# Layer norm split in two: the mean taken off a transposed copy of x, the reciprocal deviations applied to results

## The chip, the cores and the metric

The kernel runs on one core of a Trainium2 chip. TensorE (PE) multiplies matrices, VectorE (DVE), ScalarE (ACT) and GpSimd (POOL) work element by element, SyncE (SP) issues transfers. Each engine runs its own instructions in order and waits on semaphores; only transfers overlap freely. The metric is the device time of one execution in microseconds (us), the median of several runs; lower is better.

## What is computed

Two blocks, a linear attention and a gated feed-forward part with low-rank experts, read the same layer-normed tokens, and their results are added to x. There are 2048 tokens of 512 features; the feed-forward width is 1376, padded to 11 chunks of 128.

```python
def _layernorm(x, axis=-1, eps=1e-05):
    m = jnp.mean(x, axis=axis, keepdims=True)
    v = jnp.var(x, axis=axis, keepdims=True)
    return (x - m) / jnp.sqrt(v + eps)
...
xn = _layernorm(x)
# attention: Q = elu(xn Wq' + bq)+1, K likewise, V = xn Wv' + bv
out = (Q @ (K'V)) / (Q . sum(K) + 1e-8) @ Wo' + bo
# feed-forward: w = expert weights from sigmoid(xn W_router), the top 2
gate = xn @ W_gate + lora + expert_lora(w);  up = likewise
ffn = (silu(gate) * up) @ W_down + lora + expert_lora(w)
x = x + out + ffn
```

## The kernel before

Every product is made of float32 parts: an operand is rounded to a high part by ACT (`round_to`), DVE subtracts it for the low part (`sub`), and PE multiplies three times (high by high, high by low, low by high; lines 1245 to 1247).

**Stage 1** goes over 16 tiles of 128 tokens. For tile t, DVE takes mean and variance (`stats_of`, into `mv`), POOL makes the reciprocal deviation `rstd` in two instructions (`rstd_of`), and DVE writes the normed tile `xn` (`normalise`). PE turns it with four transposes (`transpose_tokens`, L1264) into one PSUM bank; ACT and DVE split that into `xt` (`tokens_hi`, `tokens_lo`), and `xt` is kept in DRAM (`scr_x`) for later stages. PE makes keys `k`, values `va` and the rest `vz`, DVE adds the key bias (`kb`), and so on. In the same tile POOL and DVE pass the expert choice of the tile before back and forth: POOL `rden` (L608), DVE `compare`, POOL `eq`, `gt`, `rank` (L611 to L615), then `rstd_of(t + 3)`, then seven small instructions up to `wtok` (L626), and `rden` of the next tile. DVE stands at `compare` until POOL's `rden` is there, and only behind it comes `tokens_lo(t + 1)`, which PE needs for the next tile.

**Queries.** Four groups of 512 tokens, each with four products `queries(g, c)` into two PSUM banks in turn. ACT reads the bank twice (`query_relus`, L757 and L759), makes an exponential (L764), and DVE adds (L1049). Then `denominators`, a DVE reciprocal of 3.35 us (`reciprocals`, L1091), ACT's rounding of it (`reciprocal_hi`), DVE's low part (`reciprocal_lo`, L1096), PE's `expand` (L1372), DVE's `scaled`, the low and high parts `qn_h`, `qn_l`, and `attention`. The last attention's products run behind the first gate product of the next stage.

**Feed-forward.** Four groups by 11 chunks: PE gate (14 products), up (14), down (14); ACT applies silu to the gate's bank, DVE multiplies by up (`hf`), and both split it.

The order of work on each engine is written out by hand; nothing reorders it.

## Time and profile before

| | |
|---|---|
| median of 3 runs | 669.52 us (669.11 to 671.9) |
| the profiled execution | 671.42 us, span 669.6 us |
| PE busy over the span | 98% |
| DVE, ACT, POOL busy | 56%, 38%, 19% |
| granted TensorE clock, mean | 0.997 |
| stage 1, queries, feed-forward end about at | 131, 228, 670 us |

A row of the timeline gives the start, the duration, engine, line, operation, output and inputs, and in brackets how long the engine had stood before it and what ended that. PE's matmuls overlap by some 0.16 us, so its pace is read from one start to the next.

### The profile page before, as it was taken

Reading aid. Unit: us, or ns where it says so; the run is one execution under the profiler, and the core shown is the slowest. Engines: PE = TensorE matmul, PEld = TensorE weight load, DVE = VectorE, ACT = ScalarE, POOL = GpSimd, SP = SyncE. Lnnn points to the kernel's source line nnn. Section 1 sums busy time; section 2 is a strip of 40 time slices with the busy share of each in tenths; the row PEclk is TensorE's granted clock in tenths of the full one; section 3 lists DMA queues with packets and bytes.
Section 4 is the critical chain, followed back from the end, with each engine's and each line's share of the span. In section 5 each row is a group of like instructions: output and inputs, shape, how many; then the busy total and the mean of one; then the engine's idle time right before and its main releaser. Section 6 shows DMA issues by size and latency. Waiting matters only on the chain.

```text
span 669.6 us, 10326 instructions
## 1 busy us (share of the span) xinstructions
PE 659.4 (98%) x3568; PEld 545.9 (82%) x3568; DVE 375.8 (56%) x698; ACT 257.5 (38%) x413; POOL 127.1 (19%) x290
## 2 busy tenths in 40 slices
PE   6999999999999999999999999999999999999998
PEld 5998999977777788888888888888888888888886
DVE  5677888778775956334345443445444326534433
ACT  4444454467235423323233333243233324323321
POOL 3466566626246230000000000000000000000000
PEclk8999999999999999999999999999999999999999
DMA  7875666644754679940025100011400001300001
GB/s 222 300 258 192 209 224 220 231 181 141 288 218 158 238 217 3 45 160 0 1 78 200 52 0 0 0 67 76 187 0 0 0 5 73 126 0 0 0 0 63
DMA packets 41642, 74.21 MB, mean 111 GB/s; under 512 B 19392, under 2 KB 20288, under 8 KB 39952
## 3 DMA queue, kind: packets, MB, share of 16 engines
q1 hardware_dynamic: 38672, 64.52, 34.6%
q10 hardware_dynamic: 2736, 9.05, 3.5%
q0 software_dynamic: 208, 0.30, 0.2%
q8 instruction: 16, 0.26, 0.2%
q14 instruction: 10, 0.08, 0.0%
HBM read 52.81 MB, written 21.04 MB: 110 GB/s over the span
## 4 chain that ended last, share of the span: by engine, by line
PE 94%; DVE 3%; DMA 1%; ACT 1%; issue 0%; SPq 0%; DVEq 0%
PE bank L1245 21%; PE bank L1246 21%; PE bank L1247 21%; PE bank L1490 18%; PE bank L1463 6%; DVE den L1091 2%; PE bank L1474 1%; PE bank L1476 1%; PE bank L1264 1%; DMA xin<-in_x 1%; PE bank L1276 1%; PE bank L1363 1%; PE bank L1501 1%; PE bank L1503 1%; PE bank L1285 0%
## 5 line engine op out<-in xcount | busy, mean ns | idle before, releaser
L1245 PE MATMUL bank<-x,up_h 128*128 128x512 f32 (+1 forms) x352 | 137.1, 390 | 0.2 <-DVE x3r L1056 0.2
L1247 PE MATMUL bank<-x,up_l 128*128 128x512 f32 (+1 forms) x352 | 137.0, 389 | 0.0
L1246 PE MATMUL bank<-x,up_h 128*128 128x512 f32 (+1 forms) x352 | 137.0, 389 | 0.0
L1182 DVE TENSOR_TENSOR hf<-bank,silu 128x512 f32<-128x512 f32 x44 | 30.4, 691 | 155.0 <-issue 135.3
L1490 PE MATMUL bank<-dn,hid_h 128*128 128x512 f32 x352 | 108.7, 390 | 0.0
L677 ACT ACTIVATE hid_h<-hf 128x512 fp32r<-128x512 f32 x44 | 27.8, 632 | 144.0 <-DVE hf L1182 144.0
L1245 PEld LDWEIGHTS bank<-x,up_h 128*128 128x128 f32 x352 | 66.1, 188 | 14.5 <-issue 0.7
L1490 PEld LDWEIGHTS bank<-dn,hid_h 128*128 128x128 f32 x352 | 65.9, 188 | 14.4 <-DVE res L1207 0.6
L1247 PEld LDWEIGHTS bank<-x,up_l 128*128 128x128 f32 x352 | 66.1, 188 | 13.8
L1246 PEld LDWEIGHTS bank<-x,up_h 128*128 128x128 f32 x352 | 66.1, 188 | 13.7
L888 DVE TENSOR_TENSOR up_l<-up_raw,up_h 128x1024 fp32r<-128x1024 f32 x44 | 54.9, 1249 | 28.1 <-ACT up_h L677 28.1
L1490 PE MATMUL bank<-dn,hid_l 128*128 128x512 f32 x176 | 68.5, 389 | 0.0
L677 ACT ACTIVATE up_h<-up_raw 128x1536 fp32r (+1 forms) x44 | 64.5, 1473 | 1.7 <-DVE qf_odd L1049 1.7
L847 ACT ACTIVATE silu<-bank 128x512 f32<-128x512 f32 x44 | 26.3, 599 | 100.4 <-PE bank L1463 100.4
L1463 PE MATMUL bank<-z,up_h 128*128 128x512 f32 x176 | 54.2, 389 | 0.0
L888 DVE TENSOR_TENSOR hid_l<-hf,hid_h 128x512 fp32r<-128x512 f32 x44 | 30.5, 692 | 33.8 <-ACT hid_h L677 33.8
L677 ACT ACTIVATE dn<-dn_raw 128x576 fp32r (+1 forms) x44 | 30.1, 684 | 31.7 <-PE bank L1476 20.6
L1245 PE MATMUL bank<-va_h,xt 128*128 128x384 f32 (+1 forms) x128 | 41.5, 324 | 0.0
L1246 PE MATMUL bank<-va_l,xt 128*128 128x384 f32 (+1 forms) x128 | 40.3, 315 | 0.0
L1247 PE MATMUL bank<-va_h,xt 128*128 128x384 f32 (+1 forms) x128 | 40.3, 315 | 0.0
L888 DVE TENSOR_TENSOR up_h<-up_raw,up_h 64x256 fp32r<-64x256 f32 x88 | 38.6, 439 | 0.6
L1490 PEld LDWEIGHTS bank<-dn,hid_l 128*128 128x128 f32 x176 | 33.0, 188 | 6.9
(166 smaller groups left out, 1083.4 us busy)
## 6 DMA issues: line engine op xcount, KB each, us to landing
x<-scr_x SPq DMA_DIRECT2D x7, 2048.0 KB, 8.5
up_raw<-in_ffn_up SPq DMA_DIRECT2D x11, 768.0 KB, 7.6
scr_x<-xt ACTq DMA_DIRECT2D x16, 512.0 KB, 4.5
xin<-in_x SPq DMA_DIRECT2D x16, 256.0 KB, 4.3
scr_z<-zt SPq DMA_DIRECT2D x16, 256.0 KB, 2.2
x3r<-in_x SPq DMA_DIRECT2D x16, 256.0 KB, 3.4
scr_att<-x3r SPq DMA_DIRECT2D x16, 256.0 KB, 2.8
...
```

Of the source, the lines that this page charges most:

```text
L677: return nc.scalar.activation(dst, src, ACT.Copy)
L847: nc.scalar.activation(silu[:], ps_g[:], ACT.Silu).then_inc(silu_done, 1)
L888: return nc.vector.tensor_tensor(dst, a, b.bitcast(F32), ALU.subtract)
L1091: nc.vector.reciprocal(den[:], den[:]).then_inc(rden_done, 1)
L1182: nc.vector.tensor_tensor(hf[:], ps_u[:], silu[:], ALU.mult).then_inc(h_done, 1)
L1245: nc.tensor.matmul(dst, lh, rh, start=start, stop=False, **kw)
L1246: nc.tensor.matmul(dst, lh, rl, start=False, stop=False, **kw)
L1247: return nc.tensor.matmul(dst, ll, rh, start=False, stop=stop, **kw)
L1264: last = nc.tensor.transpose(ps_xt[:, k * P:(k + 1) * P], xn[:, k * P:(k + 1) * P], ident[:])
L1276: last = nc.tensor.matmul(ps_kv[h * DK:(h + 1) * DK, c * AUG:(c + 1) * AUG], kf[:, s, col:col + DK], vf[:, s, c, h, :], start=(s == 0 and ...
L1463: last = nc.tensor.matmul(dst[:], up_h[:, s, col:col + P], z4[:, :, a * 2 + b, :], start=False, stop=(b == 1))
L1490: d = nc.tensor.matmul(ps_out[j][:], h[:, s, cols], w[:, s, 0:DNB - 1], start=(first and i == 0), stop=False, skip_group_check=True)
```

## The change

The host hands over x a second time, transposed (`xT`). From tile 2 on, DVE subtracts the mean from the loaded transposed tile (`centre`), with the means turned into a row by one PE transpose (`mean_rows`). `xt` now holds x minus mean. The factor `rstd` is applied later: to keys and values where they leave PSUM, to queries and gates by one more DVE product each (`query_scaled`, 16 times, `gate_scaled`, 44 times) with rows of `rstd` spread over all partitions (`rb`), and to the final results. These rows are made once: all 16 columns of `rstd` are transposed in tile 14, go to DRAM as 16 rows, and are read back with a broadcast. Every tile from 2 on loads `xT` beside x.

```diff
+                    sp.wait_ge(ln_done if isinstance(t, int) and t == 0 else ln_stats, t + 2)
                     load_x(t + 3, 1 - s)
+                    load_xt(t + 3, 1 - s)
...
+            sp.wait_ge(rrow_done, 1)
+            sp.dma_start(scr_r.rearrange("o (t p) -> (o t) p", p=P), rrow[:]).then_inc(scr_rd, 16)
+            sp.wait_ge(scr_rd, 16)
+            load_rb(rb[0][:], 0, rb_in[0])
...
                 pool.wait_ge(vare_done, t + 2)
-                nc.gpsimd.tensor_tensor(rstd[:], vare[:], mhalf[:], ALU.pow).then_inc(ln_rstd, 1)
+                nc.gpsimd.tensor_tensor(rs[:, s:s + 1], vare[:], mhalf[:], ALU.pow).then_inc(rs_done, 1)
+                pool.wait_ge(rs_done, t + 1)
+                nc.gpsimd.tensor_tensor(nrs[:, s:s + 1], rs[:, s:s + 1], minus[:], ALU.mult).then_inc(ln_rstd, 1)
+                nc.gpsimd.tensor_tensor(rstd[:, bass.ds(t, 1)], rs[:, s:s + 1], one[:], ALU.mult).then_inc(rstd_done, 1)
 
...
                 wait(act, q_done, n - 1)
-                nc.scalar.activation(qexp[:, c % 2, :], ps_q[c % 2][:], ACT.Relu, scale=-1.0,
-                                     bias=nbq[:, c:c + 1]).then_inc(qrelu_done, 1)
-                nc.scalar.activation(qf[g % 2][:, c, :], ps_q[c % 2][:], ACT.Relu, bias=bq_c[:, c:c + 1]
-                                     ).then_inc(qmax_done, 1)
+                q = qf[g % 2][:, c, :]
+                nc.scalar.activation(qexp[:, c % 2, :], q, ACT.Relu, scale=-1.0, bias=nbq[:, c:c + 1]).then_inc(qrelu_done, 1)
+                nc.scalar.activation(q, q, ACT.Relu, bias=bq_c[:, c:c + 1]).then_inc(qmax_done, 1)
...
+                nc.vector.bn_aggr(mv[:, s], stats[:]).then_inc(ln_stats, 1)
+
+            def centre(t, s, uses):
+                dve.wait_ge(xt_ready, t + 1)
+                dve.wait_ge(xtr_in[s], 16 * uses)
+                nc.vector.tensor_tensor(xtr[:, s], xtr[:, s], ps_xt[:, s * P:(s + 1) * P].unsqueeze(1).to_broadcast([P, KD, P]),
+                                        ALU.subtract).then_inc(ln_done, 1)
...
             def tokens_lo(t, s):
+                early = isinstance(t, int) and t < 2
                 dve.wait_ge(xth_done, t + 1)
-                sub(xt_l[:, s].rearrange("p k n -> p (k n)"), ps_xt[:], xt_h[:, s].rearrange("p k n -> p (k n)")
-                    ).then_inc(xtl_done, 1)
+                src = ps_xt[:].rearrange("p (k n) -> p k n", n=P) if early else xtr[:, s]
+                sub(xt_l[:, s], src, xt_h[:, s]).then_inc(xtl_done, 1)
...
-                nc.vector.tensor_tensor(kb[:], ps_k[:], bk_b[:], ALU.add).then_inc(kb_done, 1)
+                dve.wait_ge(ln_rstd, t + 1)
+                nc.vector.scalar_tensor_tensor(kb[:], ps_k[:], rs[:, s:s + 1], bk_b[:], ALU.mult, ALU.add).then_inc(kb_done, 1)
...
                     heads_of(0)
-                if ahead(t, 2):
-                    normalise(t + 2, s)
                 dve.wait_ge(vz_ready, t + 1)
                 if behind(t, 2):
                     dve.wait_ge(zst_done, t - 1)
                 nc.vector.tensor_copy(zraw[:, s], ps_z).then_inc(zraw_done, 1)
+                if ahead(t, 2):
+                    centre(t + 2, s, half + 1)
                 if first:
                     dve.wait_ge(consts_in, 64)
...
 
+            def query_scaled(g, c):
+                dve.wait_ge(q_ready, g * KD + c + 1)
+                dve.wait_ge(rb_in[g % 2], 16 * (g // 2 + 1))
+                if g > 1:
+                    dve.wait_ge(qnl_done, (g - 1) * KD)
+                nc.vector.tensor_tensor(qf[g % 2][:, c, :], ps_q[c % 2][:], rb[g % 2][:], ALU.mult).then_inc(qs_done, 1)
+
             def queries(g, cs=range(KD)):
 
                 for c in cs:
...
+                        query_scaled(g, c + 1)
                     dve.wait_ge(qmax_done, n + 1)
                     dve.wait_ge(qexp_done, n + 1)
...
             def group(g, last=False):
                 if g > 1:
+                    query_scaled(g, 1)
                     queries(g, (1, 2, 3))
...
                 scaled(g, (0, 1, 2))
                 if not last:
+                    query_scaled(g + 1, 0)
+                scaled(g, (3,))
+                if not last:
                     queries(g + 1, (0,))
-                scaled(g, (3,))
                 if last:
...
+            query_scaled(0, 1)
+            queries(0, (0,))
+            query_scaled(0, 2)
             queries(0, (1,))
             lora_weighted(TILES - 1, (TILES - 1) % 2)
             lora_lo(TILES - 2)
-            queries(0, (2,))
             dve.wait_ge(bdnh_done, 1)
             sub(bdn[0:ER, 1], bdn_raw[0:ER, 1], bdn[0:ER, 1]).then_inc(bdn_done, 1)
+            query_scaled(0, 3)
+            queries(0, (2,))
             queries(0, (3,))
             m_lo(0, (0, 1))
             reciprocals(0)
             m_lo(0, (2, 3))
+            query_scaled(1, 0)
             dve.wait_ge(bdn_done, 1)
             reciprocal_lo(0)
+            query_scaled(1, 1)
             scaled(0, (0, 1))
             queries(1, (0,))
             scaled(0, (2, 3))
+            query_scaled(1, 2)
...
 
-            def chunk(n, c, s, last=False, due=None):
+            def gate_scaled(n, g):
+                dve.wait_ge(g_ready, n + 1)
+                if isinstance(g, int) and g == 0:
+                    dve.wait_ge(rb_first_in, 16)
+                    dve.wait_ge(silu_done, 1)
+                    r = rb_first[:]
+                else:
+                    dve.wait_ge(rb_late_in, 16)
+                    r = rb_late[:, bass.ds(g - 1, 1)].rearrange("p o n -> p (o n)")
+                nc.vector.tensor_tensor(silu[:], ps_g[:], r, ALU.mult).then_inc(gs_done, 1)
+
+            def chunk(n, c, s, g, last=False, due=None):
 
                 start = isinstance(n, int) and n == 0
                 if not last and not start:
                     split_up(c + 1, 1 - s, n + 2)
-                split_dn(c, s, n + 1)
                 if due is not None:
                     due()
+                gate_scaled(n, g)
+                split_dn(c, s, n + 1)
 
...
+            def mean_rows(t, s):
+                pe.wait_ge(ln_stats, t + 1)
+                pe.wait_ge(xtl_done, 2)
+                wait(pe, ln_done, t - 1)
+                nc.tensor.transpose(ps_xt[:, s * P:(s + 1) * P], mv[:, s, 0:1].to_broadcast([P, P]), ident[:]
+                                    ).then_inc(xt_ready, 1)
...
-                if ahead(t, 1) and not first:
-                    transpose_tokens(t + 1)
...
                         ).then_inc(vz_ready, 1)
+                if ahead(t, 2):
+                    mean_rows(t + 2, s)
+                if isinstance(t, int) and t == TILES - 2:
+                    pe.wait_ge(rstd_done, TILES)
+                    nc.tensor.transpose(ps_rt, rstd[:], ident[:]).then_inc(rt_ready, 1)
                 if behind(t, 2):
...
-                    wait(pe, qmax_done, g * KD + c - 1)
+                    wait(pe, qs_done, g * KD + c - 1)
...
                 pe.wait_ge(upl_done, n + 1)
-                dst, free, ready = ((ps_g, silu_done, g_ready), (ps_u, h_done, u_ready))[a]
+                dst, free, ready, uses = ((ps_g, gs_done, g_ready, n), (ps_u, h_done, u_ready, n + 1))[a]
                 if isinstance(n, int) and n == 0:
 
-                    free, n = ((qn_done, GROUPS * KD - 1), (att_done, TILES - GT - 2))[a]
+                    free, uses = ((qn_done, GROUPS * KD), (att_done, TILES - GT - 1))[a]
                 if first:
                     pe.wait_ge(x4_in, 16 * (g + 1))
```

On POOL, in one tile of stage 1, stood these instructions (`mv` holds mean and variance, `ssum` is the expert sum):

```order
L615 TENSOR_TENSOR rank<-gt 128x8
L586 REGISTER_ALU
L587 TENSOR_TENSOR vare<-mv,epsln 128x1
L588 REGISTER_ALU
L589 TENSOR_TENSOR rstd<-vare,mhalf 128x1
L620 TENSOR_TENSOR ssum<-sel 128x4
L601 REGISTER_ALU
```

In the change there are two more, and an address computed ahead of the last:

```order
L664 TENSOR_TENSOR rank<-gt 128x8
L632 REGISTER_ALU
L633 TENSOR_TENSOR vare<-mv,epsln 128x1
L634 REGISTER_ALU
L635 TENSOR_TENSOR rs<-vare,mhalf 128x1
L637 TENSOR_TENSOR nrs<-rs,minus 128x1
L638 ISA
L638 TENSOR_TENSOR rstd<-rs,one 128x1
L669 TENSOR_TENSOR ssum<-sel 128x4
```

So behind `rank` the expert sum begins two instructions later; `vare` now belongs to tile t + 2, whose statistics are ready.

On DVE, at the reciprocal of the first query group (`m_l`: low parts of the attention matrix, `den`: denominators, `rr`: their reciprocal split), stood:

```order
L1049 TENSOR_TENSOR qf_even<-qf_even,qexp 128x512
L888 TENSOR_TENSOR m_l<-bank,m_h 128x512 x2
L1089 TENSOR_SCALAR den<-bank 128x512
L1091 RECIPROCAL den<-den 128x512
L888 TENSOR_TENSOR m_l<-bank,m_h 128x512 x2
L1096 SCALAR_TENSOR_TENSOR rr<-rr,lomask_sb,den 128x512
```

and now stands, with `rb_odd` the spread `rstd` of group 1:

```order
L1127 TENSOR_TENSOR qf_even<-qf_even,qexp 128x512 x2
L949 TENSOR_TENSOR m_l<-bank,m_h 128x512 x2
L1167 TENSOR_SCALAR den<-bank 128x512
L1169 RECIPROCAL den<-den 128x512
L949 TENSOR_TENSOR m_l<-bank,m_h 128x512 x2
L1117 TENSOR_TENSOR qf_odd<-bank,rb_odd 128x512
L1174 SCALAR_TENSOR_TENSOR rr<-rr,lomask_sb,den 128x512
L1117 TENSOR_TENSOR qf_odd<-bank,rb_odd 128x512
L1180 TENSOR_TENSOR qf_even<-qf_even,bank 128x512 x2
```

A scaling of group 1's first query has come in behind the reciprocal and two low parts, ahead of `rr`, and a second one ahead of the scaling of group 0.

ACT's order at the same place has not moved; before:

```order
L764 ACTIVATE qexp<-qexp 128x512
L677 ACTIVATE m_h<-bank 128x512 x4
L677 ACTIVATE kvt_h<-bank 128x512
L757 ACTIVATE qexp<-bank,nbq 128x512
L759 ACTIVATE qf_odd<-bank,bq_c 128x512
L764 ACTIVATE qexp<-qexp 128x512
L677 ACTIVATE rr<-den 128x512
L757 ACTIVATE qexp<-bank,nbq 128x512
L759 ACTIVATE qf_odd<-bank,bq_c 128x512
```

and in the change:

```order
L725 ACTIVATE m_h<-bank 128x512 x4
L725 ACTIVATE kvt_h<-bank 128x512
L818 ACTIVATE qexp<-qf_odd,nbq 128x512
L819 ACTIVATE qf_odd<-qf_odd,bq_c 128x512
L823 ACTIVATE qexp<-qexp 128x512
L725 ACTIVATE rr<-den 128x512
L818 ACTIVATE qexp<-qf_odd,nbq 128x512
L819 ACTIVATE qf_odd<-qf_odd,bq_c 128x512
L823 ACTIVATE qexp<-qexp 128x512
```

The two relus of group 1's first query still stand ahead of `rr`, but now read `qf_odd`, which the DVE product above writes, instead of the PSUM bank.

## Rows read from the trace of the kernel before

**Rows 1.** Busy by stretch: us, busy (count) of each engine, PEclk, DMA share, GB/s.
```profile
0.00:20.00 20.00, 14.11 (x67) 12.55 (x68) 11.34 (x25) 9.17 (x16) 6.03 (x23) 0.91 0.70 212
60.00:100.00 40.00, 40.00 (x366) 36.66 (x355) 32.58 (x106) 19.16 (x47) 25.87 (x79) 1.00 0.64 211
150.00:200.00 50.00, 49.30 (x231) 36.39 (x230) 39.61 (x46) 22.27 (x40) 22.89 (x16) 1.00 0.60 222
```

**Rows 2.** Timeline of PE, tiles 9 and 14: start us, us, what.
```profile
81.88 0.60 PE L1264 MATMUL bank<-ident_sb,xn 128*128 128x128 f32 x4
82.23 0.42 PE L1245 MATMUL bank<-va_h,xt 128*128 128x384 f32 x1
...
124.10 0.38 PE L1285 MATMUL bank<-ident_sb,zst 128*128 128x128 f32 x2
124.24 0.48 PE L1245 MATMUL bank<-wk_h,xt 128*128 128x512 f32 x1
```

**Rows 3.** Timeline of POOL in stage 1.
```profile
25.31 0.98 POOL L589 TENSOR_TENSOR rstd<-vare,mhalf 128x1 f32<-128x1 f32 x1
...
53.39 0.33 POOL L611 TENSOR_TENSOR eq<-eq,earlier_sb 128x64 f32<-128x64 f32 x1 [1.68 <-DVE eq L926]
...
54.92 0.21 POOL L615 TENSOR_TENSOR rank<-gt 128x8 f32<-128x8 f32 x1
55.33 0.65 POOL L587 TENSOR_TENSOR vare<-mv,epsln 128x1 f32<-128x1 f32 x1 [0.20 <-DVE mv L896]
56.05 0.55 POOL L589 TENSOR_TENSOR rstd<-vare,mhalf 128x1 f32<-128x1 f32 x1
...
59.19 0.20 POOL L608 TENSOR_TENSOR rden<-rexp,one 128x8 f32<-128x8 f32 x1
...
83.55 0.33 POOL L611 TENSOR_TENSOR eq<-eq,earlier_sb 128x64 f32<-128x64 f32 x1 [1.34 <-DVE eq L926]
...
89.90 0.20 POOL L608 TENSOR_TENSOR rden<-rexp,one 128x8 f32<-128x8 f32 x1
91.01 0.32 POOL L611 TENSOR_TENSOR eq<-eq,earlier_sb 128x64 f32<-128x64 f32 x1 [0.91 <-DVE eq L926]
...
121.13 0.32 POOL L611 TENSOR_TENSOR eq<-eq,earlier_sb 128x64 f32<-128x64 f32 x1 [1.03 <-DVE eq L926]
```

**Rows 4.** Timeline of DVE in stage 1.
```profile
8.13 0.69 DVE L892 BATCH_NORM_STATS2 stats<-xin 128x6 f32<-128x512 f32 x1 [2.29 <-DMA xin<-in_x]
...
55.24 0.68 DVE L975 SCALAR_TENSOR_TENSOR kf<-kb,kexp 128x512 f32<-128x512 f32 x1
56.64 0.55 DVE L901 TENSOR_SCALAR xn<-xin,mv,rstd 128x512 f32<-128x512 f32 x1 [0.71 <-POOL rstd L589]
```

**Rows 5.** Timeline of DVE, first query group.
```profile
146.17 0.69 DVE L1049 TENSOR_TENSOR qf_even<-qf_even,qexp 128x512 f32<-128x512 f32 x1 [1.76 <-ACT qexp L764]
...
148.86 3.35 DVE L1091 RECIPROCAL den<-den 128x512 f32<-128x512 f32 x1
152.13 1.22 DVE L888 TENSOR_TENSOR m_l<-bank,m_h 128x512 fp32r<-128x512 f32 x2
153.50 0.75 DVE L1096 SCALAR_TENSOR_TENSOR rr<-rr,lomask_sb,den 128x512 fp32r<-128x512 f32 x1
```

**Rows 6.** Timeline of ACT, first query group.
```profile
151.06 0.69 ACT L757 ACTIVATE qexp<-bank,nbq 128x512 f32<-128x512 f32 x1 [2.56 <-PE bank L1247]
...
152.74 0.63 ACT L677 ACTIVATE rr<-den 128x512 fp32r<-128x512 f32 x1
```

**Rows 7.** Timeline of PE, first query group and end of the last attention.
```profile
147.01 1.06 PE L1363 MATMUL bank<-qf_even,kcur 128*32 128x512 f32 x8
...
154.40 0.51 PE L1372 MATMUL bank<-rr,hrow 32*128 32x512 f32 x4 [0.43 <-DVE rr L1096]
...
245.22 0.39 PE L1245 MATMUL bank<-x,up_h 128*128 128x512 f32 x1
```

**Rows 8.** Timeline of DVE at the end of the last attention.
```profile
245.42 0.69 DVE L1056 TENSOR_TENSOR x3r<-x3r,bank 128x512 f32<-128x512 f32 x1 [2.03 <-PE bank L1247]
```

More of the change, by code:

```diff
@@ L70, with program @@
 }
-def program(nc, dram, out, scr_x, scr_z, scr_att, scr_w):
+def program(nc, dram, out, scr_x, scr_z, scr_att, scr_w, scr_r):
     ctx = ExitStack()
@@ L84, in program @@
         wtok = sb("wtok", [P, E, TILES])
+        rstd = sb("rstd", [P, TILES])
         bdn = sb("bdn", [P, 2, D], F32R)
@@ L127, in program @@
         kvt_l = at("kvt_l", [P, KD, P], F32R)
+        rb = [rb_even, at("rb_odd", [P, GN])]
+        assert place[0] <= wq_at + 4 * UPC
         place[0] = wq_at + 4 * UPC
@@ L242, in program @@
         ps_va, ps_vz = bank[4][:, 0:VA], bank[5][:, 0:P + NZ]
+        ps_rt = bank[3][0:TILES, 0:P]
         ps_z = bank[5][:, P:P + NZ]
@@ L259, in program @@
         xin_in = [sem("xin_even"), sem("xin_odd")]
+        xtr_in = [sem("xtr_even"), sem("xtr_odd")]
+        rstd_done = sem("rstd_done")
+        rs_done = sem("rs_done")
+        rt_ready = sem("rt_ready")
+        rrow_done = sem("rrow_done")
+        scr_rd = sem("scr_rd")
+        rb_in = [sem("rb_in_even"), sem("rb_in_odd")]
+        rb_first_in = sem("rb_first_in")
+        rb_late_in = sem("rb_late_in")
+        qs_done = sem("qs_done")
+        gs_done = sem("gs_done")
         ln_stats = sem("ln_stats")
@@ L602, in links, with route @@
                 return link
-            def route(t, more=True):
+            def route(t, s, more=True):
                 link = links(t)
@@ L616, in route @@
                 if more:
-                    rstd_of(t + 3)
+                    rstd_of(t + 2, s)
                 pool.wait_ge(sel_done, t + 1)
@@ L638, in _ @@
             pool.dma_start(zmask[:], dram["zmask"]).then_inc(consts_in, 16)
-            rstd_of(2)
-            with pool.Fori(0, TILES - 3) as t:
-                route(t)
-            route(TILES - 3, more=False)
+            with pool.Fori(0, TILES // 2 - 1) as p:
+                route(2 * p, 0)
+                route(2 * p + 1, 1)
             def key_sums(b):
@@ L845, in chunk @@
                     act.wait_ge(h_done, n + 1)
-                act.wait_ge(g_ready, n + 1)
-                nc.scalar.activation(silu[:], ps_g[:], ACT.Silu).then_inc(silu_done, 1)
+                act.wait_ge(gs_done, n + 1)
+                nc.scalar.activation(silu[:], silu[:], ACT.Silu).then_inc(silu_done, 1)
                 if start:
@@ L1000, in _ @@
             stats_of(0, 0, 0)
-            normalise(0, 0)
-            stats_of(1, 1, 0)
+            centre_first(0, 0)
             for k in range(KD):
@@ L1136, in _ @@
             select(TILES - 1)
-            queries(0, (0,))
+            for par in range(2):
+                dve.wait_ge(scr_xd[par], 16 * TILES // 2)
+            query_scaled(0, 0)
             key_values(TILES - 1, TILES // 2 - 1)
             heads_of(1)
+            query_scaled(0, 1)
+            queries(0, (0,))
+            query_scaled(0, 2)
             queries(0, (1,))
@@ L1157, in _ @@
             lora_lo(TILES - 1)
+            query_scaled(1, 3)
             queries(1, (2,))
@@ L1200, in results @@
                     dve.wait_ge(o_ready, g * GT + j + 1)
+                    r = rstd[:, bass.ds(g * GT + j, 1)]
                     if halves and j == GT - 1:
```

111 lines of the change are left out of this document (75 added, 36 removed).

## Prediction

> **What bounds the kernel now.** I read the stretches first, since a share over the whole span mixes stages. In 60 to 100 us, inside stage 1, PE is busy for 40.00 of 40 us, DVE for 32.58, POOL for 25.87; in 150 to 200 us, the queries, PE for 49.30 of 50 and DVE for 39.61 [rows 1]. So PE sets the time nearly everywhere, and an edit is worth what it takes from PE's list, as long as what PE waits for keeps up. That second half is where I looked next: at POOL's loop in stage 1 and at the reciprocal of the first query group, for in both the brackets of the rows are small.
>
> POOL's loop: in one tile it runs from `eq` at 53.39 to the end of `rden` at 59.39, 6.00 us; in the tiles from 8 on, where DVE also splits weights, from 83.55 to 90.10, 6.55 us. `rden` releases DVE's `compare`, and the next `eq` can start 0.91 us after it (90.10 to 91.01; there the wait bracket is 0.91, the least of the rows, against 1.68 at 53.39) [rows 3]. The loop can therefore go no faster than 6.9 us in early tiles and some 7.46 in late odd ones; the even interval behind it has a bracket of 1.34, so I take 7.36 for late tiles, a choice. The measured pace is (121.13 - 53.39)/9 = 7.53 us a tile [rows 3]. POOL is 0.2 to 0.6 us from being the bound, under an average of 65%.
>
> **Term A, stage 1.** PE loses four transposes a tile (0.35 us from 81.88 to 82.23) and gains one of 0.07 (two take 0.14 from 124.10 to 124.24) [rows 2]: 0.28 us a tile, so PE alone would go at 7.25. POOL's loop changes by four things:
> - `tokens_lo` now reads two SBUF operands, and starts at the moment POOL gets `eq`. The trace shows what such a DVE instruction does: behind `kf` (two SBUF operands, 55.24 to 55.92) POOL's one-column `vare` takes 0.65 us and ends at 55.98, just behind it, and the power instruction takes 0.98 us at 25.31 against 0.55 at 56.05 [rows 3, 4]. `eq` starts 0.15 behind `tokens_lo` (0.68 long, as `kf`), so it ends about 0.4 later.
> - `vare` need not wait for DVE (bracket 0.20) and slips in ahead of `kf`; the power instruction is then the one held, as at 25.31. Rank's end to rstd's end was 56.60 - 55.13 = 1.47 us, and becomes 0.23 + 0.98 = 1.2: 0.25 less.
> - Two more instructions. One small one is 0.20 (`rden` at 59.19) plus 0.07 to the next; the second writes a column whose address is computed first, for which I take 0.33. Together 0.6; the bounds are 0.4 (no gaps) and 1.3 (both held, 0.65 each) [rows 3].
> - `xn` (0.55, at 56.64) no longer stands beside the loop [rows 4]. I take 0.2 for it, bounds 0 and 0.4.
>
> Net +0.5 us (bounds 0 and 1.4), so the loop needs 7.4 early and 7.86 late, both above PE's 7.25: the bound passes to POOL. From tile 1's `eq` to tile 13's are 12 intervals, half early, half late: 6 x 7.41 + 6 x 7.86 = 91.6 against 12 x 7.527 = 90.3, **+1.3**. PE had some slack against this chain, but it can't use it: in tile 14 it must wait for `rstd_done` of all 16 tiles. `rstd_of(15)` ends behind `eq(13)` by 1.74 (53.39 to 55.13) + 0.4 + 1.2 + 0.6 + 0.1 = 4.05 us, while PE was there at 124.10, 2.97 behind it [rows 2, 3]: **+1.1**. The start gives back some: a statistics instruction of 0.69 us at 8.13 leaves the path to the first low part (0.3 of it, the rest was a wait for weights), one set of transposes goes before the loop begins (0.3), and two weight loads come ahead of tile 1's x, for which I take 0.5 with bounds 0 and 1 [rows 2, 4]: **-1.1**. **A = +1.3**, bounds -2 and +6. `centre` takes `normalise`'s place on DVE (0.69 as any two-operand product, for 0.55); DVE has 7.4 us a tile with no room lost, since it no longer stands 0.71 for `rstd` [rows 4]. Queued behind PE's wait in tile 14 are all keys of tile 15; SP's extra loads sit behind `xtl_done`, a full tile ahead of their use. The weights' and tables' loads behind them are not needed for tens of us.
>
> The Trainium skill has the rule behind the first of these (SBUF — State Buffer, SBUF: two separate sides): DVE and GpSimd share one pair of SBUF ports by an exclusive lock, which a DVE instruction takes when it has two SBUF inputs, or in a two-port mode, and the other engine stands for the whole of it. The trace agrees, with 0.65 and 0.98 us [rows 3]. It speaks against this change, which turns a PSUM operand into an SBUF one where POOL's chain begins; without the lock the first item would be 0 and A would be about -3.9, by 12 x 0.4 and 0.4.
>
> **Term B, the first denominators.** The add of the last query ends at 146.86 and PE's denominators begin at 147.01 [rows 5, 7]: nothing lies between. Ahead of ACT's relus there is now one DVE product of 0.69 (0.6 from start to start). **B = +0.65**, bounds 0.6 and 0.8. The loads of `rb` come before it; PE has the key-value matmuls and another query product in between, which hides them.
>
> **Term C, the first reciprocal.** Before: the reciprocal ends at 152.21 and PE's `expand` starts at 154.40, 2.19 later, through ACT's `rr` (152.74) and DVE's (153.50), in the cover of `m_l` [rows 5, 6, 7]. PE stood 0.43. Now ACT still has the two relus and the exponential of query (1, 0) ahead of `rr`, and they wait for a DVE product that stands behind the reciprocal and two `m_l`. From the reciprocal's end: 1.14 (`m_l`) + 0.66 + 0.05 + 1.68 (three ACT instructions, 151.06 to 152.74) + 0.63 (`rr`) + 0.13 + 0.75 + 0.15 = 5.2 us. **C = +3.0**, bounds 2.6 and 3.4. PE has nothing else in its queue: 3.4 us of standing. Behind it wait the scaling of group 0 and its attention.
>
> **Term D.** Query (1, 1)'s relus now begin behind `rr`, and the rounding of `qn_h` behind them; POOL's `qn_l` then ends later against PE. ACT has 1.7 us more ahead, most of it inside PE's two query products. **D = +0.3**, bounds 0 and 1.1. Groups 2 and 3 have DVE idle enough, and the scalings are placed ahead of what waits: 0.
>
> **Term E, the first gate.** PE went from the last attention straight on to the second gate product at 245.22 [rows 7]. That product now needs `gs_done` of the first, which DVE does behind the attention's last add: 245.42 + 0.69 + 0.69 + 0.13 = 246.93 [rows 8]. **E = +1.7**, bounds 1.6 and 2.0. In all other chunks the gate product has 6 us until its bank is wanted, so 43 of the 44 cost nothing; so does reading `rstd` in the results. Placing the results ahead may save PE 0.1 at three seams.
>
> **Sum.** 1.3 + 0.65 + 3.0 + 0.3 + 1.7 - 0.1 = +6.85 us. On the profiled execution's 671.42 us that is 678.3; it lies 1.9 above the median of 669.52, and against the median I predict **676.4 us**.
>
> **Rivals.**
> - **POOL keeps up**, which ends on the other side. If the lock and the two instructions cost less than POOL's slack, PE stays the bound: -1.1 - 13 x 0.28 + 1.1 = -3.6 for A, and 5.55 for the rest: 671.5 us, within 0.5%. It decides where POOL's loop needs less than 7.25 us in late tiles. For it: POOL is busy 65% [rows 1]. Against: its late loop of 7.36 is above that before anything is added. 0.22.
> - **The clock falls** in the 3.4 us of standing in C. The granted clock is 1.00, the 2.4 GHz level, in both later stretches, and 0.91 in the first 20 us, where PE worked up from standing [rows 1]. One such rise cost 0.09 x 20 = 1.8 us. That gives 678.2. For it: no row of before has PE stand that long after its start; so none speaks against. 0.18. The Trainium skill says (TensorE: Matmul & The Clock Gate, HAM oscillation) that a wait between bursts can send the clock back to its low level. No run here shows it yet.
> - **C isn't there**, as PE is late itself or ACT's relus are ready sooner, with POOL keeping up as well: 668.5, faster or the same. 0.07.
> - **POOL is held more**: both new instructions at 0.65 in every tile: A = +6, 681 us. 0.06.
> - My own case, 0.47.
>
> **How the numbers follow.** A measurement of this kernel can tell about 0.5%, 3.3 us, from no change. Slower by more (above 672.9): my case, the clock, POOL held more, and a fifth of the first rival: 0.75. Within 0.5%: the rest of that rival, and some of the third: 0.20. Faster: 0.05. The range of 670.5 to 681 leaves out the third case and the ends of A. My own case alone runs from 673.5 to 679.5.
>
> **What would show it.** Right: POOL's `eq` comes every 7.4 us early and 7.8 late, with brackets near 0.9 throughout; PE's tile 14 stands before the transpose of `rstd`; `expand` of group 0 stands 3 to 4 us behind DVE's `rr`; the second gate 1.7 us behind `gs`. Wrong: POOL's brackets stay above 1.2, and PE stays at 100% in stage 1. The prediction fails most easily in A, where 0.1 us a tile is 1.2 us, and if rows of `rstd` come so late that DVE stands at its first `query_scaled` for over 2 us.

## The result, and the profile after

The changed kernel takes 680.95 us (679.32 to 681.62), the kernel before 669.64 in the same comparison: 1.016 times as long, 95% interval 1.0147 to 1.0173. I predicted 676.4 and a range of 670.5 to 681.0, which holds it by 0.05 us. The direction was forecast, but the increase came out at 11.3 us for a forecast of 6.85.

First the stretches of the kernel after, against [rows 1], and one more that the third of them hides: us, busy (count) of PE, PEld, DVE, ACT, POOL, granted clock, DMA share, GB/s.

```profile
60.00:100.00 40.00, 39.50 (x347) 35.51 (x346) 34.27 (x106) 20.06 (x46) 29.07 (x92) 1.00 0.75 250
150.00:200.00 50.00, 45.40 (x197) 33.30 (x196) 37.51 (x46) 22.89 (x40) 21.46 (x16) 0.93 0.53 191
159.00:164.50 5.50, 5.50 (x16) 4.13 (x13) 3.09 (x6) 4.59 (x9) 3.01 (x3) 0.50 0.00 0
```

Stage 1 has lost little: PE busy for 39.50 of 40 us. The queries have lost 3.9 us of PE's time in 50, and the granted clock is 0.93 there. The last row shows where the clock fell: from 159 to 164.5 us it is 0.50, TensorE's 1.2 GHz level. What PE waited for, apart from 3.8 us for its first load, in us, times, longest:

```profile
PE bank L1486 <- DVE rr L1174: 3.8, 2, 3.4
PE bank L1375 <- DVE mv L957: 1.7, 3, 0.7
PE bank L1421 <- POOL rstd L638: 1.6, 1, 1.6
PE bank L1349 <- DVE silu L1270: 1.6, 1, 1.6
PE bank L1477 <- DVE qf_even L1127: 1.2, 1, 1.2
```

And PE's timeline at those places:

```profile
123.21 0.28 PE L1421 MATMUL bank<-ident_sb,rstd 128*16 128x128 f32 x1 [1.61 <-POOL rstd L638]
...
143.96 0.47 PE L1349 MATMUL bank<-wo_h,kvt_h 128*128 128x512 f32 x1 [0.59 <-issue]
...
148.17 1.07 PE L1477 MATMUL bank<-qf_even,kcur 128*32 128x512 f32 x8 [1.21 <-DVE qf_even L1127]
...
158.55 0.80 PE L1486 MATMUL bank<-rr,hrow 32*128 32x512 f32 x4 [3.42 <-DVE rr L1174]
...
159.87 0.63 PE L1350 MATMUL bank<-x,wq_h 128*128 128x512 f32 x1
...
160.30 0.63 PE L1351 MATMUL bank<-x,wq_l 128*128 128x512 f32 x1
...
165.14 0.40 PE L1351 MATMUL bank<-x,wq_l 128*128 128x512 f32 x1
...
255.71 0.47 PE L1349 MATMUL bank<-x,up_h 128*128 128x512 f32 x1 [1.60 <-DVE silu L1270]
```

To see where the time went I set the start of the same PE instruction in both profiles side by side:

| PE instruction | before | after | difference |
|---|---|---|---|
| keys of tile 1 | 18.86 | 18.29 | -0.57 |
| key-value products in tile 14 | 119.66 | 116.99 | -2.67 |
| transposes of `zst` in tile 14 | 124.10 | 123.32 | -0.78 |
| first attention matrices (`wo_h`) | 144.08 | 143.96 | -0.12 |
| denominators of group 0 | 147.01 | 148.17 | +1.16 |
| `expand` of group 0 | 154.40 | 158.55 | +4.15 |
| query product, 15 matmuls later | 158.15 | 165.14 | +6.99 |
| `expand` of group 3 | 227.20 | 235.93 | +8.73 |
| gate product of the second chunk | 245.22 | 255.71 | +10.49 |
| end of the span | 669.6 | 679.8 | +10.2 |

The profiled execution before lies 1.8 us above its median and that after 0.7 above its own: 10.2 + 1.8 - 0.7 = 11.3 us, the difference of the medians.

POOL in one late tile, and the `eq` two tiles on:

```profile
104.24 0.70 POOL L660 TENSOR_TENSOR eq<-eq,earlier_sb 128x64 f32<-128x64 f32 x1 [0.91 <-DVE eq L993]
...
106.31 0.19 POOL L633 TENSOR_TENSOR vare<-mv,epsln 128x1 f32<-128x1 f32 x1
106.57 0.99 POOL L635 TENSOR_TENSOR rs<-vare,mhalf 128x1 f32<-128x1 f32 x1
107.65 0.19 POOL L637 TENSOR_TENSOR nrs<-rs,minus 128x1 f32<-128x1 f32 x1
107.79 0.19 POOL L638 TENSOR_TENSOR rstd<-rs,one 128x1 f32 x1
107.93 0.20 POOL L669 TENSOR_TENSOR ssum<-sel 128x4 f32<-128x4 f32 x1
108.21 0.19 POOL L670 TENSOR_TENSOR ssum<-ssum 128x2 f32<-128x2 f32 x1
...
119.39 0.70 POOL L660 TENSOR_TENSOR eq<-eq,earlier_sb 128x64 f32<-128x64 f32 x1 [0.91 <-DVE eq L993]
```

Here is what term A was about. `eq` is held (0.70 for 0.33 us in [rows 3]), `vare` no longer, the power instruction is (0.99 for 0.55): as forecast. But `nrs`, the copy to `rstd` and the next `ssum` start 0.14 us apart, not 0.27, since none of the three waits for the one before. A late tile takes (119.39 - 104.24)/2 = 7.58 us. How this reaches PE: in late tiles it stands at the row of means for DVE's statistics, 0.50 us at 98.59 and 0.54 at 113.74.

DVE and then ACT at the first reciprocal, ACT's first row being a store's wait further up:

```profile
153.29 1.22 DVE L949 TENSOR_TENSOR m_l<-bank,m_h 128x512 fp32r<-128x512 f32 x2
154.43 0.68 DVE L1117 TENSOR_TENSOR qf_odd<-bank,rb_odd 128x512 f32<-128x512 f32 x1
157.65 0.75 DVE L1174 SCALAR_TENSOR_TENSOR rr<-rr,lomask_sb,den 128x512 fp32r<-128x512 f32 x1 [2.54 <-ACT rr L725]
```

```profile
142.15 0.65 ACT L725 ACTIVATE zt<-bank 128x256 fp32r<-128x256 f32 x2 [1.11 <-DMA scr_z<-zt]
...
155.15 0.72 ACT L818 ACTIVATE qexp<-qf_odd,nbq 128x512 f32<-128x512 f32 x1 [5.51 <-DVE qf_odd L1117]
...
156.91 0.61 ACT L725 ACTIVATE rr<-den 128x512 fp32r<-128x512 f32 x1
```

DVE's product (154.43) stands behind two `m_l`, ACT's relus (155.15) behind it, `rr` (156.91) behind them, and DVE's `rr` (157.65) last: PE's 3.42 us. It is the chain of term C, row by row. The last view is SP's queue, start and length of each issue:

```profile
128.82 0.34 SPq L512 DMA_DIRECT2D scr_r<-rrow  x1
130.19 0.34 SPq L430 DMA_DIRECT2D rb_even<-scr_r  x1
130.58 0.43 SPq L451 DMA_DIRECT2D x<-scr_x  x1
131.06 0.43 SPq L518 DMA_DIRECT2D sa_dn_sb<-in_sa_dn  x1
131.53 0.43 SPq L430 DMA_DIRECT2D rb_odd<-scr_r  x1
132.88 11.23 SPq L457 DMA_DIRECT2D scr_z<-zt  x2
```

and in the kernel before:

```profile
127.94 0.34 SPq L418 DMA_DIRECT2D x<-scr_x  x1
...
133.38 9.05 SPq L424 DMA_DIRECT2D scr_z<-zt  x2
```

SP sends the rows of `rstd` out and stands until they have landed, reads `rb_even` back, and only at 130.58 issues the 2 MB load of x, which stood at 127.94 before. The store of tile 13's `zt` (`zt` holds a tile's low-rank products) is issued at 132.88, 0.5 us sooner than before, since it waits for DVE; but it stands behind the late load and two more, and lands 9.2 us after its issue, for 4.2 before. ACT's next rounding waits for it until 142.15, 1.11 us; DVE's low part of `zt` behind it ends at 143.75. PE's attention matrices start just behind (143.96), after 0.59 us of standing.

### The profile page after: what moved, and what is told of

It is laid out like the page before. It is cut to its first block, busy times and chain, and to the rows that moved or that the text cites. A ratio compares the mean times of both kernels' runs of the same rounds, so it can differ in the third digit from the quotient of the medians.

```text
span 679.8 us, 10448 instructions
## 1 busy us (share of the span) xinstructions
PE 658.6 (97%) x3527; PEld 542.3 (80%) x3527; DVE 415.4 (61%) x758; ACT 264.8 (39%) x414; POOL 131.5 (19%) x322
## 4 chain that ended last, share of the span: by engine, by line
PE 71%; POOL 11%; DVE 6%; issue 6%; DMA 2%; ACT 2%; POOLq 1%; SPq 0%; DVEq 0%; ACTq 0%
PE bank L1604 17%; PE bank L1349 15%; PE bank L1351 14%; PE bank L1350 14%; PE bank L1577 6%; POOL rs L635 2%; PE bank L1590 1%; PE bank L1588 1%; POOL eq L660 1%; DMA scr_z<-zt 1%; DMA w_raw<-in_wvT 1%; POOL ssum L674 1%; POOL gt L663 1%; DVE den L1169 1%; POOL gt L661 1%
## 5 line engine op out<-in xcount | busy, mean ns | idle before, releaser
L908 ACT ACTIVATE silu<-silu 128x512 f32<-128x512 f32 x44 | 27.8, 633 | 153.3 <-DVE silu L1270 153.3
L1270 DVE TENSOR_TENSOR silu<-bank,rb_late 128x512 f32<-128x512 f32 x33 | 22.8, 691 | 48.7 <-PE bank L1577 48.7
L1577 PEld LDWEIGHTS bank<-z,up_h 128*128 128x128 f32 x176 | 33.0, 188 | 6.9
```

The costliest lines, as they stand in the source:

```text
L908: nc.scalar.activation(silu[:], silu[:], ACT.Silu).then_inc(silu_done, 1)
L1270: nc.vector.tensor_tensor(silu[:], ps_g[:], r, ALU.mult).then_inc(gs_done, 1)
L1577: last = nc.tensor.matmul(dst[:], up_h[:, s, col:col + P], z4[:, :, a * 2 + b, :], start=False, stop=(b == 1))
```

## The experiments

Each is the changed kernel (680.95 us) with one edit, unless it says otherwise. Ratios are to the kernel before, with their 95% intervals. The profiles compared are single executions. The median of the kernel before was 669.33 to 670.45 us from one comparison to the next, so what a gain of about 1 us is due to is read from the traces, not from the medians.

**e1_recip_first**, the reciprocal ahead of the next query:

```diff
 ACT  kvt_hi(1)
+     reciprocal_hi(0)
      queries(1, (0,))
-     reciprocal_hi(0)
 DVE  m_lo(0, (2, 3))
-     query_scaled(1, 0)
      reciprocal_lo(0)
+     query_scaled(1, 0)
```

> From the changed kernel, two lines move: ACT's rounding of the first reciprocal goes ahead of the relus of query (1, 0), and DVE's low part of it ahead of the product query_scaled(1, 0). Theory: the 3.42 us that PE stands before expand of group 0 come from that order, and the slow matmuls behind it (0.43 us from start to start instead of 0.228, from 159 to 164.5 us) come from the standing. Then the wait falls to about 0.3 us, the matmuls behind it stay at 0.228, and the time falls by 3.1 + 2.8 = 5.9 us, to about 675. Rival: the clock falls there for another reason than PE's standing (the work behind, or chance). Then 3.1 us come back alone, 677.8, and the slow stretch stays. Second rival: the wait only moves to the next bank, because queries (1, 2) now need the product later: nothing or under 1 us.

Measured: 677.59 us, 1.0122 (1.0107 to 1.0138). PE's timeline:

```profile
155.16 0.51 PE L1486 MATMUL bank<-rr,hrow 32*128 32x512 f32 x4 [0.19 <-DVE rr L1174]
...
162.41 0.47 PE L1349 MATMUL bank<-wo_h,kvt_h 128*128 128x512 f32 x1 [1.00 <-issue]
...
165.94 0.47 PE L1349 MATMUL bank<-m_h,qn_h 128*128 128x512 f32 x1 [0.55 <-POOL qn_l L713]
```

`expand` starts 3.39 us sooner and PE stands 0.19 us ahead of it; no matmul behind it is slow, and at the query product that stood at 165.14 the gain is 6.17. Then 1.0 us is given back, 5.2 at the end of the span: PE stands 1.00 us for DVE's `kvt_l` (the low part of the key-value product), which is queued behind query (1, 1) and ends at 162.31, and 0.55 for POOL's `qn_l`. So the place and the price of C are shown, and the low-clock stretch went with the wait. The median gained 3.4 us where 5.9 were expected; this profile is of an execution 1.2 us below its median, and that of the changed kernel of one 0.7 above.

**e2_busy_gap** and **e2b_busy_13**: the wait stays, but PE works in it.

```diff
             pe.wait_ge(hrow_done, 1)
+            keep_busy(ps_exp[1], 44)     (13 in e2b_busy_13)
             expand(0)
```

> From the changed kernel, 44 small matmuls of the identity by itself are put on PE ahead of expand of group 0, into a PSUM bank that expand then overwrites; nothing reads them. They fill about 3.1 of the 3.42 us that PE stands there, and DVE's rr comes no sooner. Theory (the standing lowers the clock, and the clock costs on its own): expand starts where it did, but the matmuls behind it go at 0.228 us and 2.8 us come back, about 678.1. Rival (the slow stretch isn't due to the standing): 681, as before, or slightly more. If the small matmuls held PE longer than the wait, expand would start later than 158.6 in the trace.

> The run before it overfilled the gap: a small identity matmul turned out to take 0.227 us (two passes), so 44 took 9.99 us, expand came 5.93 us late, and the 0.228 us pace behind it took 3.1 of that back. Here 13 of them stand ahead of expand of group 0, about 2.95 us for a wait of 3.42. Theory (the standing alone lowers the clock): expand starts at its old time, within 0.2 us, the query products behind it go at 0.228 us a matmul, and 2.8 to 3.1 us come back: 677.9 to 678.2. Rival: 0.4 us of standing or the kind of work is enough to lower the clock anyway: 681.

Measured: 685.27 us, 1.0233 (1.0219 to 1.0247) with 44, which fill 9.99 us and hold `expand` back by 5.93, too many; 678.12 us, 1.0121 (1.0099 to 1.0143) with 13. The second, on PE:

```profile
154.66 3.07 PE L1430 MATMUL bank<-ident_sb 128*128 128x128 f32 x26
158.15 0.51 PE L1486 MATMUL bank<-rr,hrow 32*128 32x512 f32 x4 [0.43 <-DVE rr L1174]
...
158.93 0.40 PE L1350 MATMUL bank<-x,wq_h 128*128 128x512 f32 x1
159.17 0.40 PE L1351 MATMUL bank<-x,wq_l 128*128 128x512 f32 x1
```

```profile
158.50:164.00 5.50, 5.50 (x28) 4.44 (x25) 5.47 (x10) 5.27 (x11) 2.81 (x2) 1.00 0.00 0
```

DVE's `rr` comes as late as before and `expand` starts 0.40 us from its old place (0.30 of that PE is ahead already at 151.72). But the matmuls behind it go at 0.23 us from start to start instead of 0.43, and the clock of the stretch is 1.00 instead of 0.50. The median falls by 2.83 us. That separates the two: 3.0 us are the wait, the rest is what it does to the clock. In the two profiles the gain behind `expand` is larger, 3.9 us by the denominators of group 1 (178.53 and 174.22): beside the slow matmuls themselves, 2.8 us, the small waits of group 1 have nearly gone, 0.21 us in all against 1.13.

The Trainium skill (TensorE: Matmul & The Clock Gate, HAM oscillation) says that a wait between bursts can send PE back to its low clock. The trace of the changed kernel agrees, with 0.50 behind 3.42 us of standing; it has 1.00 behind its waits of up to 1.61 us between 20 and 150 us.

**e4_gate_early**: the first gate's scaling ahead of the last attention add.

```diff
-            attention(GROUPS - 1, range(GT), ps_q)
+            attention(GROUPS - 1, range(GT - 1), ps_q)
+            gate_scaled(0, 0)
+            attention(GROUPS - 1, (GT - 1,), ps_q)
```

> From the changed kernel, DVE's gate_scaled of the first chunk goes ahead of the last of the four attention adds, where DVE stands 2.03 us anyway. Theory: the wait of 1.6 us at the second gate product is the order on DVE alone; it goes, and the time falls by 1.6 to 1.7 us, to about 679.3. Rival: the product needs the spread row of rstd or the table load of silu, which come late; then the last attention add is late instead and the wait stays, 681.

Measured: 679.29 us, 1.0143 (1.0127 to 1.0158), 1.66 less. PE's wait at the second gate is gone: from `expand` of group 3 to the end its profile is 1.7 us shorter than the changed kernel's. In DVE's timeline the product now lies where DVE stood:

```profile
251.76 0.68 DVE L1270 TENSOR_TENSOR silu<-bank,rb_first 128x512 f32<-128x512 f32 x1
```

**e6_join_later**: the transpose of `rstd`, with its wait, behind the keys of tile 15.

```diff
+                if t == TILES - 1:       (behind the keys)
-                if t == TILES - 2:       (behind vz)
                     pe.wait_ge(rstd_done, TILES)
                     nc.tensor.transpose(ps_rt, rstd[:], ident[:])
```

> From the changed kernel, PE's transpose of all rstd columns, with its wait for POOL, goes from the end of tile 14 to behind the keys of tile 15, 2.8 us of matmuls later; ACT reads it at the same place as before. Theory: the 1.61 us that PE stands there go, everything behind moves up by up to 1.6, so 679.4. Rival: the time is taken by what follows it in the trace, the low part of lora products that wait for a store on SP's queue (the first product of attention matrices stands 0.59 us for it), or DVE's chain through POOL's loop; then 0.5 us or less comes back.

Measured: 679.26 us, 1.0142 (1.0127 to 1.0158), 1.69 less. PE no longer stands there, and the instruction behind is 1.62 us sooner. Of that 0.9 is left at the first reciprocal: 0.77 went into a new wait, for `query_scaled(0, 0)`, which DVE does behind POOL's last `rank`. The rest of what its profile is ahead by, 1.1 us, lies in a shorter low-clock stretch (0.91 from 150 to 170 us, 0.83 in the changed kernel's), which isn't the edit's.

**e3_store_z_first**: on SP, `store_z(13)` ahead of the loads of `sa_dn` and `rb_odd`.

```diff
+            store_z(TILES - 3)
             sp.dma_start(sa_dn[:], dram["sa_dn"])
             sp.wait_ge(vz_ready, TILES)
             load_rb(rb[1][:], 1, rb_in[1])
-            for t in range(TILES - 3, TILES - 1):
-                store_z(t)
+            store_z(TILES - 2)
```

> From the changed kernel, SP issues the store of tile 13's lora products ahead of the loads of sa_dn and of group 1's spread rstd row, instead of behind them. Theory: the changed kernel puts the rstd rows' round trip ahead of SP's 2 MB load of x and another load ahead of this store; the store then lands at about 142.1, ACT's next rounding stands 1.11 us for it, PE's first attention matrices 0.59 us, and ACT is 0.6 us late at the first denominators beyond the 0.65 of my term B. With 0.45 MB less ahead of it the store lands 1 us sooner: ACT's wait falls under 0.3, PE's two waits (0.59 and 1.21) to about 0 and 0.7, the time by 1.0 to about 680. Rival: the 2 MB load alone sets the landing, and nothing changes (under 0.2 us).

Measured: 679.78 us, 1.0144 (1.0122 to 1.0166), 1.17 less. ACT's rounding now starts at 140.74 and stands for nothing:

```profile
140.74 0.65 ACT L725 ACTIVATE zt<-bank 128x256 fp32r<-128x256 f32 x2
```

PE's 0.59 us at the attention matrices are gone; its wait at the denominators is still 1.09 us. The store lands 8.0 us after its issue, not 9.2, so the two loads were part of it; that the 2 MB load ahead of them is the rest is not shown. From tile 14's `zst` to the denominators PE takes 0.8 us less than in the changed kernel, so of the 1.94 that B came to, 1.2 us stay: the product that I had priced at 0.65, and some 0.5 that this run does not explain. The median gained 0.4 us more than that, less than what e7_one_less, below, gained with no cause in its edit.

**e5_two_more** and **e7_one_less**: POOL's loop with two instructions more, and with one less (`nrs` made by DVE).

```diff
 e5  rstd[:, t] <- rs
+    extra[:, 0:1] <- rs
+    extra[:, 1:2] <- rs
 e7  (POOL)
-    nrs[:, s] <- rs
     (DVE, behind tokens_lo)
+    nrs[:, s] <- rs
```

> From the changed kernel, POOL gets two more one-column instructions in each tile behind the copy of rstd; nothing reads what they write. Theory (POOL's loop is the bound of stage 1's late tiles, and close to it in early ones): two times 0.25 us in each of 6 late intervals, half of it in the 5 or 6 early ones (brackets before eq are 0.2 to 0.4 above their least value there), and 0.5 at the wait for all of rstd: 3.0 + 1.2 + 0.5 = 4.7 us, 685.7. Rival (PE is the bound, as its 39.5 of 40 us busy say, and POOL has 25% of its time idle): 0 to 0.5 us, 681.

> From the changed kernel, the negated rstd is made by DVE, behind tokens_lo, instead of by POOL, so that POOL's loop has one instruction less, one column wide. Theory: late tiles go 0.25 us faster down to PE's own pace of 7.25 to 7.3 us, 6 times 0.25, and the wait for all of rstd in tile 14 falls by about 0.25: 1.7 us, 679.2. POOL's brackets before eq rise above 0.91 in late tiles. Rival: PE is the bound, or DVE's extra instruction gives it back, and nothing changes.

Measured: 684.46 us, 1.0216 (1.0191 to 1.0242), 3.5 more; and 680.08 us, 1.0143 (1.0121 to 1.0166), 0.9 less. POOL's timeline, first of e5_two_more:

```profile
111.53 0.19 POOL L640 TENSOR_TENSOR extra<-rs,one 128x1 f32<-128x1 f32 x1
111.67 0.19 POOL L641 TENSOR_TENSOR extra<-rs,one 128x1 f32<-128x1 f32 x1
111.82 0.20 POOL L672 TENSOR_TENSOR ssum<-sel 128x4 f32<-128x4 f32 x1
```

and of e7_one_less:

```profile
106.72 0.99 POOL L635 TENSOR_TENSOR rs<-vare,mhalf 128x1 f32<-128x1 f32 x1
107.88 0.19 POOL L637 TENSOR_TENSOR rstd<-rs,one 128x1 f32 x1 [0.17 <-POOL rs L635]
...
119.52 0.70 POOL L659 TENSOR_TENSOR eq<-eq,earlier_sb 128x64 f32<-128x64 f32 x1 [0.91 <-DVE eq L993]
```

With two more, a late tile takes (123.55 - 92.16)/4 = 7.85 us, against 7.57 in the changed kernel. The same loop went at 7.70 in the profiles of e3_store_z_first and e6_join_later, so two more cost between 0.15 and 0.28. PE is 4.15 us later at the transpose of `rstd`; 1.9 us of this are there by the second `eq` (31.73 against 29.86), and the rest comes in tile by tile. So POOL's loop sets the pace there, though it is busy 73% (29.07 of 40 us in the changed kernel). The brackets of `eq` are at 0.91 in nearly all tiles.

One less changed nothing that shows: (119.52 - 89.24)/4 = 7.57. The copy to `rstd` starts 0.17 us behind `rs` (106.72 + 0.99 to 107.88), a bracket that `nrs` had filled. My expectation of 0.25 an instruction was wrong for both. The 0.9 us of the median has no counterpart before the low-clock stretch, where PE is level with the changed kernel within 0.2 us; behind `expand` this profile's low-clock stretch is shorter, and 1.4 us come from that.

**e8_order_behind**: e1_recip_first, with what PE then waited for drawn forward.

```diff
 DVE
+    kvt_lo(1)
     query_scaled(1, 2)
     queries(1, (1,))
-    kvt_lo(1)
 ACT queries(1, (0,))
+    normalised_hi(0, (0, 1))
     queries(1, (1,))
-    normalised_hi(0, range(KD))
+    normalised_hi(0, (2, 3))
```

> On top of e1_recip_first: DVE's low part kvt_lo(1) goes ahead of query_scaled(1, 2) and the last add of query (1, 1), and ACT rounds the first two scaled queries of group 0 ahead of query (1, 1)'s relus. In e1_recip_first PE's waits had moved on: 1.00 us before the second attention matrices, for kvt_lo behind query (1, 1), and 0.55 before the first attention, for POOL's qn_l, which begins with ACT's qn_h. Theory: these two are what ate into the gain of e1_recip_first; both fall under 0.3, and the time falls by 1.2 more, to about 676.4. Rival: PE is held there by the matmuls' own work or by yet another producer (m_l, denominators), and less than 0.4 comes back.

Measured: 675.86 us, 1.0089 (1.0071 to 1.0108), 1.7 less than e1_recip_first by the medians, but only 0.5 less between the two profiles. Both waits are gone; a new one of 1.1 us for `m_l` (the second attention matrices' low part) stands behind them, so most of what they had cost moved on.

**e9_all**: all orders together (e8, e3, e4, e6), and ACT's rounding of `bdn` ahead of the queries.

> All of it together: the orders of e8_order_behind, SP's store of e3_store_z_first, the early first gate_scaled of e4_gate_early, the late transpose of e6_join_later, and ACT's rounding of bdn in its idle time ahead of the queries, with query_scaled(0, 3) ahead of DVE's part of bdn. If the terms add up as measured alone: 680.95 - 3.4 - 1.2 (behind) - 1.2 (store) - 1.7 (gate) - 1.7 (transpose) - 0.6 (bdn, an estimate from 1.05 us of ACT ahead of the last relus) = 671.2 us, within 0.5% of the kernel before. Rival: the waits cover each other (POOL's and SP's chains are late by themselves), and it stops at 673 or above. The third: it is faster than before, under 667.

Measured: 671.55 us, 1.0027 (1.0018 to 1.0036), within 0.4 us of the sum that was expected. In the trace, where PE still stands:

```profile
136.84 0.50 PE L1353 MATMUL bank<-x3a,wq_h 128*128 128x512 f32 x1 [0.77 <-DVE qf_even L1118]
...
166.60 1.14 PE L1514 MATMUL bank<-sb_dn_sb,sa_dn_sb 32*128 32x512 f32 x8 [1.11 <-DVE m_l L950]
```

**e10_all_more**: three orders more.

```diff
 DVE, a tile      -compare(t - 1); tokens_lo(t + 1)    +tokens_lo(t + 1); compare(t - 1)
 DVE, at the end  -select(15); query_scaled(0, 0)      +query_scaled(0, 0); select(15)
 ACT              -query_relus(1, 3); m_hi(1)          +m_hi(1); query_relus(1, 3)
```

> On top of e9_all, three orders more. (1) DVE does tokens_lo ahead of compare, where it stands 0.3 to 0.6 us for rden, so that POOL's eq and the gt behind it are no longer held (0.70 and 0.41 us against 0.33 and 0.32): if POOL's loop sets the pace of stage 1, late tiles go from 7.57 to about 7.3 us, 1.8 us in all. (2) query_scaled(0, 0) goes ahead of the last select, where DVE stands 0.72 us: PE's wait of 0.77 us goes. (3) ACT rounds the second attention matrices ahead of query (1, 3)'s relus: PE's wait of 1.11 us for m_l goes. Sum: 671.55 - 1.8 - 0.8 - 1.1 = 667.9 us, just under the kernel before. Rival for (1): DVE itself is full (7.0 of 7.57 us), compare comes 0.3 us later instead, and the pace stays at 7.5 or more; then 669.5 us. Rival for (2) and (3): the waits move to the next producer, and it stays at 671.

Measured: 671.65 us, 1.0023 (1.0014 to 1.0032): nothing against e9_all, where 3.7 us were expected. POOL in one late tile:

```profile
104.56 0.33 POOL L660 TENSOR_TENSOR eq<-eq,earlier_sb 128x64 f32<-128x64 f32 x1 [0.91 <-DVE eq L994]
...
110.43 0.74 POOL L675 TENSOR_TENSOR wtok<-sel,ssum 128x8 f32 x1 [0.17 <-POOL ssum L674]
```

`eq` is free (0.33), but now `wtok` is held (0.74 for 0.21): DVE's instruction of two SBUF operands still falls into the loop. The Trainium skill (SBUF — State Buffer, SBUF: two separate sides) describes an exclusive lock; the trace agrees, with the hold moved from `eq` to `wtok`, not gone. A late tile takes (119.57 - 89.67)/4 = 7.48 us, for 7.57 in the changed kernel and 7.70 in e9_all. PE's wait for `query_scaled(0, 0)` is gone, that for `m_l` is not (1.1 us). This profile is 1.0 us shorter than that of e9_all, though the medians of 12 executions each are level.

**e0_before_again**: the kernel before, unchanged.

> The kernel before, unchanged. Its first profile has the granted clock at 0.74 from 8 to 13 us, its other executions are in part 2 us shorter. Theory: the clock's dip at the start belongs to that execution, not to the kernel; an execution without it begins the keys of tile 1 some 1.8 us sooner than 18.86 us, and takes 669 to 669.7 us. Then the start of the changed kernel is no gain against the median of before. Rival: the dip is in every execution, and the time is 671.

Measured: 669.34 us. From 8 to 13 us, first of the profile shown in [rows 1], then of this one:

```profile
8.00:13.00 5.00, 2.73 (x7) 2.17 (x8) 4.83 (x10) 4.61 (x9) 3.35 (x6) 0.74 1.01 373
```

```profile
8.00:13.00 5.00, 4.44 (x19) 3.28 (x19) 4.62 (x8) 3.86 (x7) 3.14 (x6) 1.00 1.04 367
```

The clock's fall at the start, 0.74, is that execution's, not the kernel's. Here tile 1's keys start at 16.75 us, against 18.86 in the first profile and 18.29 in the changed kernel's. So against an undisturbed start the change loses 1.5 us by there. From there on the two profiles of the kernel before keep the same distance, 2.1 us, to the end.

## Why the prediction was right, and where it was not

The direction was right, and two terms of the sum, C and E. That the range holds the result is luck: its upper end of 681 was the price of POOL being held more, which did not happen, and my own case ran only to 679.5. By the two profiles the sum is 10.2 us for 6.85, and the errors in it partly cancelled: A came out 2.1 us below its term (-0.8 for +1.3), B, the clock and D together 5.6 above theirs. The other 1.1 us up to the 11.3 of the medians come from the executions that were profiled. Against e0's profile, whose start is undisturbed, A is +1.3, its own number, and that is luck too: it is made of +1.5 at the start, -2.1 in the loop and +1.9 at the join.

Terms against the two profiles, in us, where the join is PE's wait for all of `rstd` in tile 14; the last column names what bears on it.

| term | predicted | measured | |
|---|---|---|---|
| A, start | -1.1 | -0.6 | e0: +1.5 against an undisturbed start |
| A, loop and join | +1.3 + 1.1 | -2.1 + 1.9 | e5, e7, e6 |
| B, first denominators | +0.65 | +1.94 | e3, in part |
| C, first reciprocal | +3.0 | +3.0 | e1 |
| the clock behind C | 0 (a rival: +1.8) | +2.8 in this execution | e2b, e1 |
| D | +0.3 | +1.7 | e2b, in part |
| E, first gate | +1.7 | +1.8 | e4 |
| results | -0.1 | -0.3 | |
| sum | +6.85 | +10.2 | |

**Right.** C and E: both were read as orders on one engine, with the durations of the rows, and both came to 0.1 us, in place and price. The direction follows from them alone. The lock in A is in the rows as stated.

**A**: the mechanism of the loop held, two sizes did not. I gave the two new instructions 0.6 us a tile, 0.27 and 0.33 to the next; they take 0.28, since they wait for nothing on each other. That is 0.3 in each of six late intervals, 1.8 us, and 0.3 at the join. The early tiles went at 7.34 us for my 7.41. Late ones took 7.57 for 7.86, above PE's own 7.25, so there the loop, and not PE, set the pace, as e5 bears out, and PE's 0.28 us less a tile brought nothing. Up to tile 14 PE gained 2.1 us where I had it lose 1.3, and lost 1.9 at the join. I read the two as one thing: the join is paced by POOL, and gives back what PE had run ahead; e6 shows the wait, no run shows that link. The start was wrong as a step: I compared with a profile whose clock had fallen, though its 0.91 stood in [rows 1], and booked part of that as a gain of the change; I did not price PE's waits for the statistics ahead of the rows of means: 0.7 us at 18.18, at the first of them, and 0.5 each at 98.59 and 113.74.

**B** failed in the sentence that the loads of `rb` are hidden. They are, themselves; what they are queued ahead of on SP is not. The x load went 2.6 us later, the store behind it landed 9.2 us after its issue for 4.2, and ACT stands 1.11 us for the store. I had named this kind of cost for the stage's weights and looked no further down the queue.

**The clock** was the rival, at 0.18, where it should have been the case: the 3.4 us of standing that I forecast were the condition it needed. Its price was 2.8 in this execution, not 1.8, as `expand` and then 5.3 us of query products (159.28 to 164.56) went at half pace, 0.43 us a matmul. It is not a constant: in e7_one_less, with the same wait of 3.42 us, it is 1.4 less. The rival's price came from the first 20 us of a profile whose clock had fallen there by chance, as e0 shows.

**D** was under-priced: 1.3 us more in group 1, in small waits (0.15 at the second attention matrices, 0.29 for `m_l`, 0.69 for `dn_raw`, down weights to which DVE adds a low-rank product), and 0.4 at `expand` of group 3, where I had put 0 for groups 2 and 3. Its bound was 1.1. In e2b_busy_13, at full clock, the waits of group 1 are 0.21 in all, so most of them came with the slow stretch and belong to the clock; the 0.41 in group 3 is there too. What ends the waits is DVE's and ACT's order, but e8's orders moved them more than they removed them.

The orders drawn forward bring the change to 671.55 us, 0.3% above the kernel before. Where the rest is can be read by setting e9_all's profile against e0's, the undisturbed one. PE starts tile 1's keys 1.3 us late, but at tile 14's `zst` it is level (121.82 and 122.02). By the first denominators it is 1.8 us behind (146.64 and 144.88), at `expand` of group 1 3.0 (177.86 and 174.88), at the end of the span 3.0. So it lies between tile 14 and the denominators, where the wait of 0.77 us is, and in group 1, where that of 1.11 us is, and not in the late tiles. No run took it away: e10 removed the first wait and the medians stayed.
